# Three rounded-half products for the projections of the 32-wide layer, and an arena shared by two layers

## The reference

```python
x = ln(x + L0(x, adj))   # attention, 4 heads of 64, masked softmax
x = ln(x + L1(x, adj))   # 4 heads of 256: tanh(mask(scores)) @ Wh, then a gate
x = ln(x + L2(x, adj))   # 8 heads of 32, see below
x = ln(x + L3(x, adj))   # attention as L0
# L2, the 32-wide layer:
m = embs @ map_w.T + map_b
n = m / norm(m) per head;  cos_adj = (n @ n.T > 0.1)
q = m @ q_w.T + q_b;  k = m @ k_w.T + k_b
p = softmax(mask(q @ k.T / sqrt(32))) * keep
adj = cos_adj * p
sem = embs @ gcn_map_w.T + gcn_map_b
out = relu(((adj @ sem) @ gcn_W.T) / (adj.sum(-1) + 1))
```

## Time and profile before

| | |
|---|---|
| median of 3 runs | 3054.45 us |
| profiled execution | 3052.91 us, of which the span is 3051.1 us |
| TensorE matmul (PE) | busy 2698.6 us, 88% |
| weight load (PEld) | 2375.4 us, 78% |
| VectorE (DVE) | 1928.8 us, 63% |
| ScalarE (ACT) | 1398.1 us, 46% |
| GpSimd (POOL) | 994.0 us, 33% |
[...]

### The profile page before, as it was taken

One profiled execution on the slowest core, in us unless ns is written; L12 is line 12 of the kernel. 1 busy time (PEld: TensorE's weight loads), 2 busy tenths in 40 slices (PEclk: granted clock), 3 DMA queues, 4 the chain that ended last, 5 costly groups with the idle time before them and its releaser, 6 DMA issues. The chain is left out here.

```text
span 3051.1 us, 60430 instructions
## 1 busy us (share of the span) xinstructions
PE 2698.6 (88%) x21265; PEld 2375.4 (78%) x21265; DVE 1928.8 (63%) x6525; ACT 1398.1 (46%) x3841; POOL 994.0 (33%) x1067
## 2 busy tenths in 40 slices
PE   4789989899998989999989999899999998999985
PEld 4777888778788877778877778887777887777874
DVE  3356666666666666666666666667666666666664
ACT  0234454554455454445455445545444545544542
POOL 0123333333333323333333333332333333333331
PEclk9799999999999999999999999999999999999997
DMA  3000000000000000000000000000000000000000
GB/s 112 5 5 10 2 9 9 8 9 9 9 1 9 9 8 9 9 1 9 9 8 9 9 9 1 9 9 8 9 9 1 9 9 8 9 9 9 1 5 7
DMA packets 44470, 29.63 MB, mean 10 GB/s; under 512 B 21264, under 2 KB 44048, under 8 KB 44432
## 3 DMA queue, kind: packets, MB, share of 16 engines
q1 hardware_dynamic: 44432, 29.13, 3.2%
HBM read 20.73 MB, written 8.39 MB: 10 GB/s over the span
## 5 line engine op out<-in xcount | busy, mean ns | idle before, releaser
L1413 POOL TENSOR_TENSOR a32r<-a,a32r 128x512 fp32r<-128x512 f32 x128 | 164.2, 1283 | 664.0 <-ACT a32r L1063 664.0
L204 PE MATMUL bank<-a32r 128*128 128x256 f32 x1024 | 309.2, 302 | 69.1 <-DVE a32r L1204 27.0
L138 POOL TENSOR_SCALAR l_ve<-l_mv 128x2 f32<-128x2 f32 x128 | 29.3, 229 | 878.7 <-DVE l_mv L123 878.7
L204 PEld LDWEIGHTS bank<-a32r 128*128 128x128 f32 x1024 | 197.1, 192 | 124.4 <-DVE a32r L1204 71.9
L205 PE MATMUL bank<-a32r 128*128 128x256 f32 x1024 | 291.7, 285 | 0.0
L206 PE MATMUL bank<-a32r 128*128 128x256 f32 x1024 | 291.5, 285 | 0.0
L1135 ACT ACTIVATE b<-b,s_sh 128x256 f32<-128x256 f32 x512 | 252.4, 500 | 5.6 <-DVE s_sh L335 5.6
L1408 POOL TENSOR_TENSOR a32r<-a,a32r 128x512 fp32r<-128x512 f32 x128 | 163.4, 1276 | 255.6 <-ACT a32r L1067 255.6
L1204 DVE SCALAR_TENSOR_TENSOR a32r<-bank,g_b_z,a32r 128x256 fp32r<-128x256 f32 x256 | 112.1, 479 | 184.2 <-ACT a32r L1044 184.2
L1304 DVE SCALAR_TENSOR_TENSOR b<-bank,b 128x256 f32<-128x256 f32 x512 | 196.5, 422 | 44.9 <-ACT b L1135 37.1
L335 DVE CUSTOM_DVE_ANT_0 b<-bank,s_add 128x256 f32<-128x256 f32 x512 | 181.5, 420 | 42.8 <-PE bank L962 40.9
(11 more groups left out here) (246 smaller groups left out, 8891.8 us busy)
## 6 DMA issues: line engine op xcount, KB each, us to landing
x_in<-in_x SPq DMA_DIRECT2D x32, 256.0 KB, 2.8
out<-x SPq DMA_DIRECT2D x32, 256.0 KB, 2.1
adj_a<-in_adj SPq DMA_DIRECT2D x32, 64.0 KB, 2.5
adj_b<-in_adj SPq DMA_DIRECT2D x32, 64.0 KB, 1.9
b<-in_L_gnn_A_w SPq DMA_DIRECT2D x1, 1024.0 KB, 7.6
a<-in_L_gnn_W SPq DMA_DIRECT2D x4, 256.0 KB, 4.5
a<-in_L_gnn_attn SPq DMA_DIRECT2D x4, 256.0 KB, 4.1
g_b_wh<-in_L_gnn_bW SPq DMA_DIRECT2D x1, 512.0 KB, 8.2
```

What stands on the lines that cost most here:

```text
L204: pe.matmul(out, w[0], x[0], start=first, stop=False)
L1413: pool.tensor_tensor(G.am[h % 2][1], G.th[:, h % 2, :, :], G.am[h % 2][0].bitcast(F32), ALU.subtract).then_inc(G.a.sem, 1)
```

## The change

S's input and its four projection weights become pairs, so that the 16 fp32 matmuls of a round become 48 of fp32r. ScalarE's copy in b_x_t writes the hi half; VectorE gets a new dve_lower in b_x_t for the lo half, and the projections wait for that one. At setup the four weights are halved, which takes two VectorE operations each in place of one copy. To make room, a32 shrinks from 10 places to 5: A's probabilities, their transposes, q, k, v, and the setup's attn, fc, g1 and the constant ones move to places of the arena that the fp32r places of G use later in the round. The arena is allocated once in fp32 and once in fp32r at the same address. S.xt moves from place 7 of b32 to a tensor of its own. No other semaphore is added or taken away.

```diff
+ARENA, ARENA_AT = 22, 16512
+        arena = sb("arena", [P, ARENA * T * NODES])
+        arena_r = nc.alloc_sbuf_tensor_at("arena_r", [P, ARENA * T * NODES], F32R, offset=ARENA_AT)
...
-        a32, a32r = places("a32", 10, F32), places("a32r", 22, F32R)
-        b32 = places("b32", 13, F32)
-        x1 = a32(9)
+        a32, a32r, plain = places("a32", 5, F32), places_of(arena_r), places_of(arena)
+        b32, b32r = places("b32", 13, F32), places("b32r", 2, F32R)
+        x1 = a32(4)
...
-        A.e, A.pt, A.qt, A.kt, A.v, A.xb = a32(0, 4), a32(4, 4), a32(4), a32(5), a32(8), x1
+        A.e, A.pt, A.qt, A.kt, A.v, A.xb = plain(10, 4), plain(16, 4), plain(14), plain(15), plain(8), x1
...
-        S.x_t_psum, S.x_t_sb = signal("l2_x_t_psum"), signal("l2_x_t_sb")
+        S.x_t_psum, S.x_t_hi, S.x_t_sb = signal("l2_x_t_psum"), signal("l2_x_t_hi"), signal("l2_x_t_sb")
...
-        S.m, S.sq, S.u, S.xt, S.sem = (b32(n) for n in (4, 5, 6, 7, 0))
+        S.m, S.sq, S.u, S.sem = (b32(n) for n in (4, 5, 6, 0))
+        S.xt = split(b32r, 0)
...
-        S.w_m, S.w_q, S.w_k, S.w_s = (sb(f"s_w_{n}", [P, T, DIM])[:, :, :] for n in "mqks")
+        S.w_m, S.w_q, S.w_k, S.w_s = (split_sb(f"s_w_{n}", [P, T, DIM]) for n in "mqks")
...
-        W.w, W.attn, W.r = a32(0, 4), a32(4, 4), b32(0, 4)
+        C.ones = plain(20)[:, 0, 0:P]
+        W.w, W.attn, W.r = a32(0, 4), plain(10, 4), b32(0, 4)
...
             def slot_b(stage, g):          # ScalarE
                 if stage == "b_x_t":
                     act.wait_ge(S.x_t_psum.sem, S.x_t_psum.at(g))
-                    act.activation(S.xt, view(BB[2]), ACT.Copy).then_inc(S.x_t_sb.sem, 1)
+                    act.activation(S.xt[0], view(BB[2]), ACT.Copy).then_inc(S.x_t_hi.sem, 1)
...
             def slot_b(stage, g):          # VectorE
-                if stage == "b_project":
+                if stage == "b_x_t":
+                    dve.wait_ge(S.x_t_hi.sem, S.x_t_hi.at(g))
+                    dve_lower(dve, BB[2], S.xt).then_inc(S.x_t_sb.sem, 1)
+                elif stage == "b_project":
```

More of the change, by code:

```diff
@@ L430, in build @@
         C.ident, C.ident_bf = sb("ident", [P, P]), sb("ident_bf", [P, P], BF16)
-        C.ones, C.minus_one, C.minus_half = sb("ones", [P, P]), sb("minus_one", [P, 16]), sb("minus_half", [P, 16])
+        C.minus_one, C.minus_half = sb("minus_one", [P, 16]), sb("minus_half", [P, 16])
         x_in, x_loaded = sb("x_in", [P, T, DIM]), signal("x_loaded", 16)
@@ L445, in places, with places_of @@
         def places(name, count, dt):
-            t = sb(name, [P, count * PLACE], dt)
+            return places_of(sb(name, [P, count * PLACE], dt))
+        def places_of(t):
             def at(first, n=1):
@@ L544, in build @@
         W = Names()
-        W.w, W.attn, W.r = a32(0, 4), a32(4, 4), b32(0, 4)
+        C.ones = plain(20)[:, 0, 0:P]
+        W.w, W.attn, W.r = a32(0, 4), plain(10, 4), b32(0, 4)
         W.a_w = b32(0, 4).rearrange("p h t n -> p (h t n)").rearrange("p (t n) -> p t n", t=T)
-        W.fc, W.g1, W.g2, W.map, W.q, W.k, W.gm = a32(8), a32(9), b32(4), b32(5), b32(6), b32(7), b32(8)
+        W.fc, W.g1, W.g2, W.map, W.q, W.k, W.gm = plain(8), plain(9), b32(4), b32(5), b32(6), b32(7), b32(8)
         W.g1_t, W.q_t, W.k_t = W.g1, W.q, W.k
@@ L660, in c_bias @@
                 for kc in range(T):
-                    last = pe.matmul(b[:, 0:HG], C.ones[:, :], W.ab[:, kc, :], start=(kc == 0), stop=(kc == T - 1))
+                    last = pe.matmul(b[:, 0:HG], C.ones, W.ab[:, kc, :], start=(kc == 0), stop=(kc == T - 1))
                 return last
@@ L691, in dve_setup @@
             for jt in range(T):
-                dve.tensor_scalar(W.gb_rows[:, jt, :], C.ones[:, :], W.gb[:, jt:jt + 1], None, ALU.mult)
+                dve.tensor_scalar(W.gb_rows[:, jt, :], C.ones, W.gb[:, jt:jt + 1], None, ALU.mult)
             for h in range(HG):
@@ L1396, in _ @@
             pool.memset(C.minus_half[:, :], -0.5).then_inc(const_ready, 1)
-            pool.memset(C.ones[:, :], 1.0).then_inc(const_ready, 1)
+            pool.memset(C.ones, 1.0).then_inc(const_ready, 1)
             pool.wait_ge(const_ready, 3)
```

## The result

The changed kernel takes 3124.22 us (median of 4 runs, 3120.84 to 3125.28) against 3055.76 us of the kernel before beside it (3052.01 to 3057.09): ratio 1.0224, 95% interval 1.0206 to 1.0242. It is slower, as forecast, but by 68 us and not by 24.5; 3124 lies outside the range of 3054 to 3098.

What follows compares the result with a forecast made beforehand. Bound: the VectorE and GpSimd chain ahead of b_unit_t, and the granted clock. From 3052.91 us: products 0, clock +23.4, setup +1.4, last round -0.3, giving 3077.4; median 1.54 above, so 3079; range 3054 to 3098.

Steps and rivals of the forecast that it cites:

- the mechanism and its sign: Ahead of b_unit_t: saved PE time only lengthens the wait, the clock falls more often behind it, kernel slower by 24.5 us.
- The products: S's projections: PE saves 1.20 us a round, but b_unit_t begins where it did; gain 0, bounds 0 and 1.20 a round.
- cover: In b_x_t, VectorE's idle time left behind the new operation before L330's wait for ScalarE ends: 1.3 us, so cost 0.
- The arena: A's tensors only change addresses: cost 0, bounds within 0.2 us a round, 6 us either way.
- The price of one fall: Clock at 0.50 behind b_unit_t delays the round by 1.3 us, taken between 0.77 read and 1.71 at most.
- I take 23 of 30, that is 18 rounds more: Falls behind b_unit_t go from 5 to 23 of 30 full rounds; bounds 0 and 25 more; cost 23.4 us.
- rival 3: Clock falls every round at the worst place, or later stretches fall more often too: +42.8 + 1.1 = 3098; chance 0.12.
- one fall priced per round: Clock term behind b_unit_t: 18 more rounds with one fall of 1.3 us each, 23.4 us, bounds 0 and 42.8.
- The setup: Second VectorE operation for each of four weights, two of them delaying PE: 1.4 us, bounds 0 and 2.8.
- The two waits named: Setup: PE's waits at 62.56 (q_t and k_t, behind w_m) and 70.67 (a copy, behind w_k), 0.69 us longer each.
- The inner range of 3062 to 3093: The forecast's own range, from 10 to 25 more falls at 0.77 to 1.55 us each.
- A longer wait, more falls: Ahead of b_unit_t: wait grows from 1.61 to 2.81 us, so falls behind it go from 5 to 23 of 30 rounds.

Runs made afterwards that it cites:

- the arena alone: Changed kernel with S's projections as before, one fp32 tensor each side and no new VectorE operation, so only the arena is left: 3063.57 us, ratio 1.0022.
- The kernel with the second falls filled: Changed kernel with 2 matmuls of nobody's use only ahead of head 0's scores in g_1: 3096.49 us, ratio 1.0128.

## Why the prediction was wrong

**Right: the mechanism and its sign.** The products gain nothing: b_unit_t's wait was to be 2.81 us and is 2.9; full-clock rounds are 89.06 us with halves and 89.07 without. L1347 (L1336 before) waited for a product only once in the run, 0.7 us. The new L331 stands under idle time: it starts at 1576.60, and the L331 behind it waits until 1578.49 for ScalarE, 1.20 us of cover, forecast 1.3. The 48 matmuls end at 1589.82 - 2.96 = 1586.86, 5.86 us after the first, where the 16 took 7.07 to the same point: 1.21 saved, forecast 1.20. The arena: no change in the length of a round without falls. The price of one fall, forecast 1.3 us, is 12.88 - 11.52 = 1.36; that it came so close is luck in part, since 1.3 was a choice between 0.77 and 1.71 and no reading.

**Wrong: "I take 23 of 30, that is 18 rounds more".** It was 29 of 29, 24 more. I treated each wait as a draw with a chance that grows with its length. The prediction itself had read that the same few lengths of rounds return again and again: a warning that nothing in them is drawn. From the round of 731.70 on, those of before follow two sequences, of about 90.9, 90.0 and of 89.0, 90.6, 90.0. A fall moves what is behind it: L336 is 1.36 us late in the round of 1581.00. That the shift goes on into the next round, and that in the changed kernel a round with its falls so ends as it began, is my estimate from the counts of 29 of 29, and no run shows it. What is shown is the 92.16 us from one first fall to the next, always, in the changed kernel and in those with two and three matmuls left out, though their work differs. The kernel with 0.86 us added ahead of g_gate has the same mean round (92.17) and the same wait, and 9 falls, so the wait's length alone doesn't set the count. What makes 92.16 us the length that they keep, no run tells. The table's step between 2.0 and 2.5 us could not be read from the profile of before, but that the count could be 29 could; I had it only in rival 3, at 0.12.

**Wrong: one fall priced per round.** The prediction's sum has one fall of 1.3 us a round. The rows of after have three, two of them more often than before: g_1 from 5 to 23 and d_probs from 22 to 29. The prices can be read from the round of 1581.00 against the one of 1544.20. It is 1.36 us late at L336; at L988, behind the second fall, 24.69 - 21.87 = 2.82, of which part comes back; 2.44 at d_probs; and 92.20 - 89.05 = 3.15 at its end. So the first fall costs 1.36, the second 1.08 and the third 0.71. By the counts that is 24 x 1.36 = 33 us for the new first falls, 5 x (1.36 - 0.77) = 3 because the five of before got dearer as well, 18 x 1.08 = 19 for the second and 7 x 0.71 = 5 for the third: 60 of the 61.5 us measured. This is an estimate from one round. The kernel with the second falls filled doesn't price them alone: its mean round is 0.87 us shorter (91.28 for 92.16), but it also has 7 third falls fewer and 8 more of the long first stretches. Rival 3 did name "the later stretches fall more often as well", but its 3098 is again one fall a round, 42.8; with the second falls it would have been about 3118, with the third 3123. So the right case was named and its price forgot a good part of it.

**Small.** The setup was to cost 1.4 us, with 2.8 as the bound, and costs 2.06: L661 before and L669 after do the same.

```profile
91.94 0.99 PE L661 MATMUL bank<-n_ab,ones 128*128 128x4 f32 x4
```

```profile
94.00 0.99 PE L669 MATMUL bank<-n_ab,arena 128*128 128x4 f32 x4
```

The two waits named did grow, from 3.92 to 4.65 us and from 0.87 to 1.60, but PE came 0.7 us earlier to the first, so that behind it only 0.05 us are lost (62.61 for 62.56), and 1.29 behind the second (71.96 for 70.67). The last 0.8 us appear later, in matmuls ahead of which the trace shows no wait; their cause stays open. The inner range of 3062 to 3093 had left the setup out, 1.1 us at either end.

**A longer wait, more falls.** The prediction took this from 23 of 30 against 5 of 30. It holds here in its sign: 5 falls at 1.6 us, 29 at 2.5. It gives no count, though: from 1.6 to 2.0 us nothing changed (5 and 5 of 29), and 2.9 us had 29 falls in the changed kernel and 9 with 0.86 us of work added elsewhere.

**Open.** Why 2.0 us is harmless and 2.5 us is not; why the kernel with 4 fills ahead of g_gate alternates, and why the clock of its runs differs from 0.936 to 0.949; why the arena alone has a little less clock. Leaving matmuls out makes the wait longer and the work ahead of it less, fills do the opposite, and no run here changes one without the other. Not tried: GpSimd's power moved earlier so that the wait itself goes, and the changed kernel with all three fills.

## What to carry to other kernels

TensorE work taken from ahead of a wait that stays (1.2 us a round) gave nothing here and cost 68 us: first look what ends the wait, then whether the clock falls behind it. The rounds of this loop do the same, and the first falls came every 92.16 us in three kernels: price also the case in which every round has the fall, and let the later ones fall more often too, rather than multiplying a chance by a price. Where a wait can't be shortened, a few matmuls that nobody reads were worth 1.1% here (some 32 us), nearly the 38 us that the change could have saved at most.

## What the chip showed that I had not expected

- Two matmuls fewer per round, 0.86 us of less work, made the kernel 2.1% slower; one fewer made no difference (ratio 0.9995).
- Added work paid: 12 fills a round (5.2 us of PE) made the changed kernel faster by 94 us, 3124.22 to 3030.5.
- 2 fills in a place where PE had no wait, 26 us of work over the run, left the time at 3123.96 beside 3124.22: fewer falls paid for them (58 for 81).
- In three kernels whose work in the round differs (the change; two and three matmuls left out), the fall behind b_unit_t came every 92.16 us, 28 times out of 28.
- An fp32r matmul of 128x256 steps at 0.119 us, an fp32 one at 0.432, both at PEclk 1.00: three for one save 17%.
